# Decoder layer on one core: where rounding, clip, low parts and weight loads stand in their engines' order

## What is computed

```python
x = _layernorm(x + attn(x, qkvw, qkvb, ow, ob))      # 32 heads of 32, softmax(q k^T / sqrt(32)) v, then ow
q1 = fake_quant(x, x1_scale, x1_zp)                  # round(x / s + z), clip to 0..255, (q - z) * s
q2 = fake_quant(ctx_4096, x2_scale, x2_zp)           # the context, 2 x 1024 x 1024
x = _layernorm(x + matmul(q1, q2))
x = _layernorm(x + ffn(x, W_base, b_base, W_router, A, B))   # dense 1024 x 1024 plus top-2 of 8 low-rank experts
```

## Time and profile before

| | |
|---|---|
| three runs | 709.98, 710.16, 711.01 us (median 710.16) |
| the profiled execution | 711.73 us, of which the span of the trace is 709.9 |
| PE busy | 694.6 us, 98% of the span, 3489 matmuls |
| DVE, ACT, POOL busy | 468.7 (66%), 416.8 (59%), 289.4 (41%) |
| the chain that ended last | 90% PE, 3% issue, 3% SP, 2% DMA, 2% DVE |
| granted clock of PE | 0.998 over the span |

### The profile page before, as it was taken

One profiled execution on the slowest core, in us unless ns is written; L12 is line 12 of the kernel. 1 busy time (PEld: TensorE's weight loads), 2 busy tenths in 40 slices (PEclk: granted clock), 3 DMA queues, 4 the chain that ended last, 5 costly groups with the idle time before them and its releaser, 6 DMA issues.

```text
span 709.9 us, 11767 instructions
## 1 busy us (share of the span) xinstructions
PE 694.6 (98%) x3489; PEld 527.0 (74%) x3496; DVE 468.7 (66%) x833; ACT 416.8 (59%) x807; POOL 289.4 (41%) x209
## 2 busy tenths in 40 slices
PE   6999999999999999999999999999999999999996
PEld 5777778777787787787777877866767777888885
DVE  6887466575585575665755756567688679785574
ACT  5458577685685685776856856864567672221111
POOL 6692180171162153134126149836644734131130
PEclk9999999999999999999999999999999999999999
DMA  8656436346345444543643475755824332131101
GB/s 288 190 173 218 128 79 205 86 120 198 89 119 154 131 119 131 157 116 97 193 117 87 122 231 149 234 186 187 279 96 166 120 119 90 60 148 59 60 30 60
DMA packets 55956, 99.20 MB, mean 140 GB/s; under 512 B 11008, under 2 KB 21632, under 8 KB 55024
## 3 DMA queue, kind: packets, MB, share of 16 engines
q1 hardware_dynamic: 55632, 98.36, 45.2%
q10 hardware_dynamic: 288, 0.39, 0.2%
HBM read 56.41 MB, written 16.65 MB: 103 GB/s over the span
## 4 chain that ended last, share of the span: by engine, by line
PE 90%; issue 3%; SPq 3%; DMA 2%; DVE 2%; ACT 0%; POOL 0%; POOLq 0%; DVEq 0%
PE bank L482 57%; PE st_pair L612 8%; PE bank L626 8%; PE bank L582 7%; SPq L265 2%; PE bank L733 2%; PE st_pair L733 2%; PE st_pair L759 2%; PE st_pair L482 2%; PE bank L535 1%; DMA c_raw<-in_ctx 1%; DMA qp<-m_row 1%; PE bank L748 1%; PE bank L718 1%; DMA big_raw<-in_xT 0%
## 5 line engine op out<-in xcount | busy, mean ns | idle before, releaser
L1446 DVE TENSOR_REDUCE columns<-bank 128x1 f32<-128x512 f32 x256 | 172.9, 687 | 77.7 <-PE bank L582 77.2
L904 ACT ACTIVATE bank<-bank,columns 128x512 f32<-128x512 f32 x256 | 169.2, 661 | 31.2 <-DVE columns L1446 29.3
L899 ACT ACTIVATE probs<-st_pair 128x1024 f32<-128x1024 f32 x112 | 114.9, 1025 | 95.0 <-PE st_pair L612 94.2
L482 PE MATMUL bank<-big_hi,w_hi 128*128 128x512 f32 x368 | 146.0, 397 | 6.1 <-DVE big_lo L1338 6.1
L482 PE MATMUL bank<-big_hi,w_lo 128*128 128x512 f32 x368 | 144.2, 392 | 0.0
L482 PE MATMUL bank<-big_lo,w_hi 128*128 128x512 f32 x368 | 144.2, 392 | 0.0
L582 PE MATMUL bank<-kp,qp 128*128 128x512 f32 (+1 forms) x256 | 100.6, 393 | 1.6 <-ACT bank L904 1.5
L612 PE MATMUL st_pair<-qp,kp 128*128 128x512 f32 x256 | 86.1, 392 | 0.5 <-ACT probs L899 0.4
L1175 POOL TENSOR_SCALAR c_raw<-c_raw,sc 128x1024 f32<-128x1024 f32 x16 | 19.2, 1202 | 164.0 <-DMA c_raw<-in_ctx 160.3
L482 PEld LDWEIGHTS bank<-big_hi,w_hi 128*128 128x128 f32 x368 | 69.7, 189 | 20.1 <-DVE big_lo L1338 6.1
L482 PEld LDWEIGHTS bank<-big_hi,w_lo 128*128 128x128 f32 x368 | 69.6, 189 | 14.9
(11 more groups left out here) (183 smaller groups left out, 1128.0 us busy)
## 6 DMA issues: line engine op xcount, KB each, us to landing
w_raw<-in_wqkv SPq DMA_DIRECT2D x7, 1536.0 KB, 9.0
c_raw<-in_ctx SPq DMA_DIRECT2D x16, 512.0 KB, 4.0
qp<-q_hi SPq DMA_DIRECT2D x128, 64.0 KB
kp<-k_hi SPq DMA_DIRECT2D x124, 64.0 KB
big_raw<-in_xT SPq DMA_DIRECT2D x16, 256.0 KB, 5.6
qp<-q_lo SPq DMA_DIRECT2D x64, 64.0 KB
c_scratch<-c_q SPq DMA_DIRECT2D x16, 256.0 KB, 2.2
r_all<-r_scratch SPq DMA_DIRECT2D x64, 64.0 KB, 2.0
```

What stands on the lines that cost most here:

```text
L482: mm = nc.tensor.matmul(dst, lhs[a], rhs[b], start=(k == 0 and n == 0) if first is None else False, stop=(k == last_k and n == 2))
L899: nc.scalar.activation(probs[:, j, t:t + 2, :].rearrange("p t q -> p (t q)"), st_pair[:, :], ACT.Exp).then_inc(sem["exp_ok"], 2)
L904: nc.scalar.activation(bank(max_bank(s, n)), bank(max_bank(s, n)), ACT.Exp, bias=m_col[:, n:n + 1], accum_out=l_col[:, 1 - par, n:n + 1]). ...
L1446: nc.vector.reduce_max(m_col[:, n:n + 1], bank(max_bank(s, n)), AX, negate=True).then_inc(sem["rowmax"], 1)
```

## The change

Five pieces:

1. **Rounding at the step's end.** In steps 2 to 14 DVE rounds the context tile behind the step's last small copy, where before it did so behind row maximum 13. Step 15 keeps its place, behind 13.
2. **Clip of steps 1 and 2.** In step 1 POOL clips the step's tile right behind its scaling, in place of DVE. In step 2 DVE clips at the step's end, not behind row maximum 8.
3. **Low parts.** In steps 1 and 2 the low parts of q and k come one row maximum later, behind n = 6 and 12; the high parts stay.
4. **Output weights.** `load_ow` in steps 14 and 15 is issued behind all packing of heads 2 and 3.
5. **After step 15.** The first load of the quantised context goes behind the spreading of the last reciprocals, and the last maxima are written before the wait for the transposed scores.

```diff
                 if maxima:
                     store_shift(s, par)
-                if isinstance(s, int) and s >= UNITS - 2:
-                    load_ow(s + 2 - UNITS, 3 * s + 3)
                 if proj:
                     pack(s, par, 2, "k")
                     if 3 not in early:
                         pack(s, par, 3, "q")
                     pack(s, par, 3, "k")
+                if isinstance(s, int) and s >= UNITS - 2:
+                    load_ow(s + 2 - UNITS, 3 * s + 3)
...
-            load_c2(0)
+            store_shift(UNITS, 0)
             sp.wait_ge(sem["st_mm"], NS * (UNITS - 1))
             load_residual(0)
-            store_shift(UNITS, 0)
-
-
             store_recip(UNITS - 1)
             spread_recip(UNITS - 1)
+            load_c2(0)
             load_residual(1)
...
+                    if second:
+                        pool.wait_ge(sem["ctxq_1"], 2)
+                        pool.wait_ge(sem["ctxq_2"], 1)
+                        nc.gpsimd.tensor_scalar(c_raw[:, :], c_raw[:, :], 0.0, QMAX, ALU.max, ALU.min).then_inc(sem["ctxq_2"], 1)
...
                     if proj and n in (5, 11):
-                        low(0 if n == 5 else 1)
-                    if proj and n == 8 and not begin and not second:
+                        low_hi(0 if n == 5 else 1)
+                    if proj and n in ((6, 12) if early else (5, 11)):
+                        low_lo(0 if n == (6 if early else 5) else 1)
+                    if proj and n == 8 and not begin and not early:
                         clip_context(s)
...
-                    if proj and n == 13 and not begin and not second:
+                    if n == 13 and isinstance(s, int) and s == UNITS - 1:
                         round_context(s)
...
                 if maxima and proj:
                     copy_recip(s - 1)
+                if isinstance(s, int) and s == 2:
+                    clip_context(s)
+                if proj and not begin and not second and not (isinstance(s, int) and s == UNITS - 1):
+                    round_context(s)
                 if second:
-                    clip_context(s)
+                    dve.wait_ge(sem["c2_out"], 16)
                     round_context(s)
```

More of the change, by code:

```diff
@@ L366, in step @@
                     pack(s, par, 3, "k")
+                if isinstance(s, int) and s >= UNITS - 2:
+                    load_ow(s + 2 - UNITS, 3 * s + 3)
+                if proj:
                     if begin:
@@ L1397, in step, with low_hi @@
                 begin = isinstance(s, int) and s == 0
-                def low(piece):
-                    hi, lo = ((q_hi, q_lo), (k_hi, k_lo))[piece]
+                def low_hi(piece):
+                    hi = (q_hi, k_hi)[piece]
                     wait_alone(dve, sem["proj_done"], 3 * s + piece + 1)
@@ L1407, in low, with low_lo @@
                                             bias[:, bass.ds(g, 1), piece:piece + 1].rearrange("p a b -> p (a b)"), None, ALU.add).then_inc(sem["hi_ok"], 1)
+                def low_lo(piece):
+                    hi, lo = ((q_hi, q_lo), (k_hi, k_lo))[piece]
                     wait_alone(dve, sem["hi_ok"], 2 * s + piece + 1)
```

## The result

The changed kernel takes **717.36 us** (median of 6 runs, 716.75 to 719.34); the kernel before, with more runs than the prediction had, 710.59 us (6 runs). The ratio is **1.0101, interval 1.0087 to 1.0114**: slower by 7.2 us. The forecast was 715.1 us in a range of 712.6 to 718.0. The direction, the place and the chain of waits were right; the size was 2.3 us short, because the fall of PE's clock behind the stop was kept as a rival and not put into the sum, and because one of the gains was read from a stretch that differs between executions. Two single executions among the experiments, of 1180 and 1773 us, are disturbed ones and are left out of every median.

A forecast was written before the change was run, and what follows sets the result against it. PE, busy for 98% of the span, was taken as the bound, so only its idle time counts. The terms -0.4 - 1.2 + 4.6 + 2.1 - 0.2 = +4.9 us, added to 710.16, gave 715.1 us, range 712.6 to 718.0.

The forecast's parts named there:

- the chain of waits: Step 15: weights issued 6.2 us later delay POOL's split and scaling, then DVE's clip 5.9 us, then PE 4.2 us.
- Piece 4, step 15: Late output weights hold DVE's clip and PE in step 15: +4.6 us, bounds +3.5 and +5.9.
- rival C: PE's clock falls behind the 4.2 us hold in step 15: 2.1 us more, 717.2 us; chance 0.17.
- the prediction's own sign for C: Behind the hold in step 15, PE's matmuls 0.4 us apart would show that the clock fell.
- The way to +4.6: Step 15 ends with DVE's last maximum, at 440.9 instead of 436.27, behind clip, seven maxima, k's parts and rounding.
- Piece 4, step 16: Second half of the weights 10.2 us later, PE 4.6 later, margin 3.4: +2.1 us, bounds +1.0 and +2.8.
- Rival B: Step 15's delay gives SP and POOL time in step 16, so only the first hold counts: 713.0 us; chance 0.17.
- Piece 1: Rounding at the step's end fits into DVE's wait for PE: -0.4 us, bounds 0 to -0.5.
- step 5's excess: Step 5 takes 28.3 us against 27.9 undisturbed; moving the rounding wins these 0.4 us.
- Pieces 2 and 3: Steps 1 and 2: 2.1 us won in step 2, of which part is kept: -1.2 us, ends 0 and -2.1.
- The give-back forecast for that place: Step 3's first transposed score waits for the maxima's DMA, so only 1.5 of step 2's 2.1 us can be kept.
- Piece 5: After step 15, PE has the last maxima at once: -0.2 us; the moved 2 MB load taken as 0, bounds 0 and +1.

The follow-up runs named there:

- e5: The changed kernel, both output-weight loads late, but POOL scales step 15's context tile ahead of the first split of output weights: 721.31 us, ratio 1.0145.
- e4_load15: The changed kernel with only step 15's output-weight load late, step 14's load back in its old place: 712.15 us, ratio 1.0022.
- the first execution: The kernel before, unchanged, in the profiled execution that the prediction read: 711.73 us.
- e7: The kernel before with POOL clipping in step 1 and DVE clipping and rounding at the end of step 2, nothing else: 710.59 us, ratio 0.9999.
- e1_load_back: The changed kernel with the output-weight load back ahead of the last ten packing DMAs in steps 14 and 15: 709.17 us, ratio 0.9979.

## Why the prediction came out as it did, point by point

**Piece 4, step 15: +4.6 forecast, +6.25 measured.** The chain of the prediction is the one in the trace, link by link: POOL idle for 9.87 us where "about 10 or more" was said, DVE 6.00 where 5.9 was, PE's stop 4.78 where 4.2 was. Two terms are off. The stop is 0.6 longer, because the landing took 5.59 us instead of 5.4, and the clip 1.09 instead of 0.7. And the step that failed: the sum puts the clock at nothing. Its 1.7 us stood as rival C, with 2.1 us and a chance of 0.17, and the prediction's own sign for C (matmuls 0.4 us apart behind the hold) is there. C comes on top of the forecast, and it happened in the trace of each of the six kernels in which PE was idle for over 2 us (2.21 to 4.62). (The Trainium skill, "TensorE: Matmul & The Clock Gate", section on HAM oscillation, describes this for matmul groups behind waits for a DMA; these traces agree, with matmuls 0.43 us apart behind each such stop.) That C's number, 717.2, lies 0.2 us from the measured median is partly luck: its clock term was 0.4 too large and its base, 710.16, 0.4 too small. The way to +4.6 was wrong as well, though its size was near: I had the step end with DVE's last maximum, held by the clip, k's parts and the rounding. In the trace PE, at the lower clock, was the slower one, and DVE waited for it (the last maxima stand behind idle times of 0.83 and 0.69 us). The terms that make the step are PE's: 4.8 of stop and 1.7 of clock, less the 0.2 us that the old step already had.

**What the step-15 reading left out** is the tile's own landing behind the weights. It changed nothing in the sum, since POOL's split hid it by 1.4 us, but I named one releaser where there were two, and so built e5 on a wrong cure.

**Piece 4, step 16: +2.1 forecast, +2.31 measured**; the second load 10.2 us later by the forecast; 9.4 in the traces, with PE 3.7 later. That the step-15 hold only partly pays for it, as forecast, e4_load15 shows with 2.9 where there is no hold. Rival B is out.

**Piece 1: -0.4 forecast, -1.0 measured alone, with 0.1 to 1.8 possible.** The step that failed, as far as the traces show, is "step 5's excess is all that is won". The rounding is long or short by what POOL does beside it (1.15 us in step 3 of the first execution, 2.76 in e7). In every case looked at it ended 0.55 us behind POOL's split: issued at 95.48 beside a split that ended at 97.69, it ended at 98.24 (e7); issued at 154.38 beside one that ended at 155.51, it ended at 156.06. The Trainium skill, "SBUF — State Buffer", section "Who interferes with whom", has a rule for it: a VectorE instruction in a two-port mode and a GpSimd instruction lock each other out for a whole instruction. These rows agree, but for the 0.73 us that the rounding takes alone, of which only 0.55 come behind the split.

**Pieces 2 and 3: -1.2 forecast; no gain that their own runs can tell.** The pair of profiled executions shows -2.1 up to the end of step 2, none of it given back at step 3's first transposed score (it starts at 78.17, and SP's row began at 67.16 instead of 68.24). The give-back forecast for that place does show in e4_load15, where PE waits there for the maxima's DMA and step 3 takes 28.5 us. The step that failed lies ahead of both: the stops of the earlier trace rows were taken as the kernel's own in every execution, when they hang on when a load lands in the crowded first 60 us, and two of five executions have them. A warning was on the page: the profiled execution was 1.6 us slower than the median, and the gains read in it were still taken off the median. Pieces 1, 2, 3 and 5 together are worth 1.2 us between the medians (e1_load_back), and the forecast had 1.8, which the interval, 0.9 to 2.1, doesn't exclude.

**Piece 5: -0.2 forecast**, -0.34 between the two profiled executions; 0 to 0.5 by the others.

**The sum.** e1_load_back to the changed kernel is 709.17 to 717.36, so piece 4 costs 8.2 us of medians, where 6.7 was forecast; the 1.7 us of clock are about the difference. Gains 0.6 smaller and losses 1.5 larger make the 2.1 us by which 4.9 fell short of 7 (7.2 by the ratio, 6.8 between the medians). The range held because its upper end was C.

**Left open.** Why the lower clock lasts for seven matmuls in some executions and thirteen in others; the changed kernel's own runs spread over 2.6 us, which would fit. Whether it falls in every run. And how the gain of piece 1 divides over steps 3, 5 and 7: the excess of step 3 is 0 to 1.2 us and that of step 5 0.1 to 0.8, with no rule that these traces show.

## What to carry to other kernels

When a load is moved behind other work, list everything that stands behind it in three places: on the queue that issues it, on the engine that consumes it, and in the DMA engines' backlog, where here the small load issued behind the 2 MB took 10.2 us to land and not 4.0. In these traces a stop in which PE was idle for 2.2 us or more cost more than itself, because the matmuls behind it ran at half speed: add this to the stop and don't keep it as an alternative. And a gain that sits in the crowded start of a program is to be believed only from several executions; one profile of the kernel before had 2.6 us there that the next one hadn't.

## What was not expected of the hardware

- The same DVE instruction (the rounding of a 128 x 1024 tile) took 0.73 us alone and 1.15, 1.68, 2.07 and 2.76 us beside POOL's splits. Each time it ended 0.55 us behind POOL's 2.4 us instruction, whenever in it it had been issued.
- The clock fell behind PE's idle times of 2.21, 3.18 and 4.03 to 4.62 us, and did not behind 1.62 and 1.47; behind each fall 7 to 13 matmuls ran at 0.43 us, and the whole slow stretch took 1.7 to 3.0 us more than at 0.23 us a matmul.
- A 512 KB load issued 1.8 us behind a 2 MB one landed 10.2 us after its issue, and 3.7 us after it when issued ahead of it.
